# Four stages of a one-core transformer kernel recut: expert scaling on ScalarE, a convolution as TensorE products, and two reordered tails

## What is computed

```python
# layer 6: one of 8 experts per token
probs = softmax(xt @ router_w + router_b)
gate, idx = max(probs), argmax(probs)
y = gate[:, None] * (xt @ expert_w[idx] + expert_b[idx])

# layer 7: a memory trained by gradients along the sequence, chunks of 64 tokens
k, v, q = (causal_dwconv(hidden @ W.T, taps, bias) for each of three)   # 4 taps, 32 channels each
alpha, eta, theta = (mean over 32 gates of sigmoid or softplus) per token
per chunk: g = grad of |silu(k @ W1.T) @ W2.T - v|^2 at the chunk's start, clipped to norm 1
           S = eta*S - theta*g;  W = (1 - alpha)*W + S       # scan over the tokens
           retrieved = silu(q @ W1t.T) @ W2t.T
out = rmsnorm(retrieved @ Wo.T) * norm_g * (hidden @ gW.T + gb)
```

## Time and profile before

| | us |
|---|---|
| median of 3 runs | 3037.89 |
| lowest, highest | 3034.91, 3043.79 |
| the profiled execution | 3041.35 |
| its span (first to last instruction) | 3039.6 |
| busy over the span: TensorE, VectorE, ScalarE, GpSimd | 2865.2, 2198.7, 1436.9, 762.3 |
| stage l2_ffn | 53.4 |
| stage l3_prepare | 47.0 |
| stage l3_scan | 183.0 |
| stage l3_output | 22.9 |

### The profile page before, as it was taken

How to read it: one execution, slowest core, us unless ns; L and a number is a source line. 1 busy time by engine, 2 the same in 40 slices (tenths; PEclk the granted TensorE clock), 3 DMA queues, 4 the chain that set the end, 5 groups by cost and what they waited for, 6 DMA issues and landing times. The chain is left out here.

```text
span 3039.6 us, 43162 instructions
## 1 busy us (share of the span) xinstructions
PE 2865.2 (94%) x15588; PEld 1781.1 (59%) x15588; DVE 2198.7 (72%) x4611; ACT 1436.9 (47%) x2774; POOL 762.3 (25%) x680
## 2 busy tenths in 40 slices
PE   6999999999976999999999999999999887799698
PEld 4666666666643555555555555555555444466587
DVE  6888888888836877777777777777776467766655
ACT  3666666666641344444444444444444330433343
POOL 1000000000000344444444444444444310066200
PEclk7999999999996899999999999999999898655599
DMA  4121212121005011111101111101110000000000
GB/s 100 28 53 27 53 27 53 27 53 22 1 10 126 1 42 42 42 42 29 35 22 42 42 42 36 35 18 39 42 42 1 33 8 8 6 2 2 18 1 15
DMA packets 45476, 96.39 MB, mean 32 GB/s; under 512 B 13440, under 2 KB 33488, under 8 KB 37072
## 3 DMA queue, kind: packets, MB, share of 16 engines
q1 hardware_dynamic: 45264, 93.63, 13.5%
HBM read 35.67 MB, written 7.34 MB: 14 GB/s over the span
## 5 line engine op out<-in xcount | busy, mean ns | idle before, releaser
L963 ACT ACTIVATE l1a_PT<-l1a_st 128x512 f32<-128x512 f32 x1024 | 596.6, 598 | 760.7 <-PE l1a_st L879 756.5
L980 DVE TENSOR_REDUCE l1a_m<-l1a_aux 128x1 f32<-128x512 f32 x1024 | 667.0, 685 | 125.9 <-PE l1a_aux L841 123.8
L930 POOL TENSOR_TENSOR l1a_acc<-l1a_acc,l1a_PT 128x1024 f32<-128x1024 f32 x224 | 570.2, 2546 | 680.2 <-ACT l1a_PT L963 680.2
L465 DVE TENSOR_REDUCE l0s_mquad<-l0s_mx 128x1 f32<-128x512 f32 x1024 | 635.5, 683 | 142.7 <-PE l0s_mx L350 142.7
L440 ACT ACTIVATE l0s_PT<-l0s_st 128x512 f32<-128x512 f32 x1024 | 529.1, 602 | 274.3 <-PE l0s_st L366 271.6
L892 PE MATMUL l1a_ov<-l1a_PT,l1a_V 128*64 128x512 f32 x2048 | 495.7, 605 | 0.0
L877 PE MATMUL l1a_st<-l1a_QA,l1a_KA 128*128 128x512 f32 x1024 | 447.3, 437 | 2.3 <-issue 2.3
L366 PE MATMUL l0s_st<-l_QS,l_KS 128*128 128x512 f32 x1024 | 438.5, 431 | 5.3 <-DMA l_QS<-l0s_mrow 2.7
L350 PE MATMUL l0s_mx<-l_KS,l_QS 120*128 120x512 f32 x1024 | 417.7, 414 | 7.1 <-DMA l_QS<-qk_rows 7.0
L879 PE MATMUL l1a_st<-l1a_QB,l1a_KB 65*128 65x512 f32 x1024 | 405.9, 396 | 0.0
L841 PE MATMUL l1a_aux<-l1a_KA,l1a_QA 128*128 128x512 f32 x1024 | 399.0, 438 | 0.8 <-DVE l1a_lo L992 0.8
(11 more groups left out here) (349 smaller groups left out, 2642.4 us busy)
## 6 DMA issues: line engine op xcount, KB each, us to landing
l1a_KA<-l1a_hi SPq DMA_DIRECT2D x32, 512.0 KB, 8.2
l_KS<-qk_rows SPq DMA_DIRECT2D x64, 192.0 KB
l_QS<-qk_rows SPq DMA_DIRECT2D x128, 96.0 KB
l1a_QA<-l1a_hi SPq DMA_DIRECT2D x16, 512.0 KB, 4.5
l1a_QA<-l1a_lo SPq DMA_DIRECT2D x16, 512.0 KB, 8.6
l1a_QB<-l1a_hi SPq DMA_DIRECT2D x16, 512.0 KB, 4.5
l1a_KB<-l1a_lo SPq DMA_DIRECT2D x16, 512.0 KB, 6.4
qk_rows<-l0s_hi SPq DMA_DIRECT2D x64, 64.0 KB, 5.3
```

The lines of the kernel that those rows point to most:

```text
L465: nc.vector.tensor_reduce(mquad[:, u % 2, tile, g:g + 1], mx[:, n % MX0, :], axis=AX.X, op=ALU.max).then_inc(mx_free[n % MX0], 1)
L930: nc.gpsimd.tensor_tensor(acc[:, h % 2, 1, :], first, PT[:, g % PT_SLOTS, :], ALU.add).then_inc(added_pool, 1)
L963: nc.scalar.activation(PT[:, g % PT_SLOTS, (u % 2) * CW:(u % 2 + 1) * CW], st[:, u % ST1, :], ACT.Exp, scale=1.0 / float(np.sqrt(HD1))).th ...
L980: nc.vector.tensor_reduce(m4[:, b, q, c:c + 1], src, axis=AX.X, op=ALU.max).then_inc(aux_read, 1)
```

## The change

**l2_ffn.** The mask is made with a reduction and comparisons over all tiles at once instead of `max` and `max_index` per tile. The eight experts of a tile are split: four (`pv`) are added into X by VectorE as before, four (`pa`) are scaled by ScalarE into SBUF (`part`), and VectorE adds these in four wide additions per group. Six half-tiles are multiplied ahead of the mask instead of four.

```diff
-                for t in range(NT):
-                    nc.vector.max(top[:, t, :], probs[:, t, :]).then_inc(topped, 1)
-                for t in range(NT):
-                    dve.wait_ge(topped, t + 1)
-                    nc.vector.max_index(index[:, t, :], top[:, t, :], probs[:, t, :]).then_inc(topped, 1)
...
+                link(nc.vector.tensor_reduce(rowmax[:, :], probs[:, :, :], axis=AX.X, op=ALU.max))
+                link(nc.vector.tensor_tensor(e[:, :, :], probs[:, :, :], over_experts(rowmax[:, :]), ALU.is_lt))
+                link(nc.vector.scalar_tensor_tensor(e[:, :, :], e[:, :, :], float(E8), over_tokens(expert_no[:, :]),
+                                                    op0=ALU.mult, op1=ALU.add))
+                link(nc.vector.tensor_reduce(first[:, :], e[:, :, :], axis=AX.X, op=ALU.min))
...
+                    for i in range(HALF):
+                        nc.scalar.activation(part[:, c % 2, i, t % TPC, :], pa[:, t % 2, i * D:(i + 1) * D], ACT.Copy,
+                                             scale=mask[:, t, HALF + i:HALF + i + 1]).then_inc(scaled, 1)
...
+                        dve.wait_ge(scaled, HALF * TPC * (c + 1))
+                        for i in range(HALF):
...
+                            nc.vector.tensor_tensor(x, x, tiles(part[:, c % 2, i, :, :]), ALU.add).then_inc(summed, 1)
```

```diff
+            def convolve(c):
+                pe.wait_ge(taps_done, 1)
+                pe.wait_ge(eta_done, 2 * (c + 1))
+                nc.tensor.matmul(pb[0:R3, c, :], wt[:, TAPS - 1, :], xnT[:, cols(c)], start=True, stop=False)
+                for back in range(1, TAPS):
...
+            def rate():
+                pe.wait_ge(ln_done, 1)
+                pe.wait_ge(gate_read, 2)
...
-            nc.scalar.activation(gate_half[:, :], cw[:, 0:1], ACT.Tanh)
...
             nc.scalar.activation(T["Eend"][:, :], chunks(T["E"][MAIN, :])[:, :, CHUNK - 1], ACT.Copy)
+            nc.scalar.activation(gate_half[:, :], cw[:, 0:1], ACT.Tanh)
...
-            nc.gpsimd.tensor_tensor(ksq[:, :, :], T["ktok"][:, :, :], T["ktok"][:, :, :], ALU.mult).then_inc(ksq_done, 1)
```

```diff
                     nc.tensor.matmul(pred, state[:, c % 4, 1, 0, :], hd[:, c % 3, :], start=True, stop=True
                                      ).then_inc(s["pred_full"], 1)
                     if c >= 1:
-                        pe.wait_ge(s["tok_done"], 3 * c)
-                    if c >= 2:
-                        pe.wait_ge(s["m2_ready"], c - 1)
-                    nc.tensor.transpose(htok, hd[:, c % 3, :], ident[0:DM, 0:DM]).then_inc(s["htok_full"], 1)
+                        second_half_y1(c - 1)
...
                     nc.scalar.activation(e1[:, :], z, ACT.Tanh, scale=0.5).then_inc(s["e1_done"], 1)
...
+                    nc.scalar.activation(rest[:, :], e1[:, :], ACT.Identity, scale=-0.25, bias=quarter[:, :]
+                                         ).then_inc(s["rest_done"], 1)
...
+                    nc.scalar.activation(ckq[:, c % 2, :], T["CKQ"][:, at(c)], ACT.Copy, scale=thU[:, c:c + 1]
+                                         ).then_inc(s["ckq_done"], 1)
```

```diff
+            def gate(c):
+                dve.wait_ge(ms_done, TPC * (c + 1))
+                nc.vector.tensor_tensor(o[:, TPC * c:TPC * (c + 1), :], po[:, c, :].rearrange("p (t d) -> p t d", d=D),
+                                        T["gate"][:, TPC * c:TPC * (c + 1), :], ALU.mult).then_inc(gated, 1)
...
+                        nc.vector.scalar_tensor_tensor(X[:, t, :], o[:, t, :], inv[:, t:t + 1], X[:, t, :],
+                                                       op0=ALU.mult, op1=ALU.add).then_inc(added, 1)
-                    nc.vector.tensor_tensor(xt, xt, ot, ALU.add).then_inc(added, 1)
```

More of the change, by code:

```diff
@@ L1483, in l2_ffn @@
         norm(load)
+        HALF = E8 // 2
         probs = sb("probs", [P, NT, E8])
@@ L1579, in _ @@
                 dve.wait_ge(mask_done, 1)
                 adds = 0
[L1581 to L1585, removed]
+                for t in range(0, NT, 2):
+                    dve.wait_ge(pv_full, t + 2)
                     for i in range(HALF):
                         for j in range(2):
-                            t = units[u + j][0]
@@ L2100, in _ @@
             act.wait_ge(d1_set, 1)
             eta_of(0)
-            project(2)
+            gates(2)
             eta_of(1)
-            project(3)
+            convolved(0)
+            gates(3)
             eta_of(2)
+            act.wait_ge(tanh_done, NC)
+            nc.scalar.activation(tn[low, :], tn[low, :], ACT.Abs).then_inc(abs_done, 1)
+            convolved(1)
             eta_of(3)
-            for c in range(NC - 1):
-                query(c)
+            act.wait_ge(half_set, 1)
@@ L2109, in _ @@
+            act.wait_ge(abs_done, 1)
+            nc.scalar.activation(soft[3 * DM:4 * DM, :], tn[low, :], ACT.Ln, scale=0.5, bias=half[low, :]).then_inc(ln_done, 1)
             move(0)
-            for c in range(NC - 1):
-                value(c)
-            query(NC - 1)
-            act.wait_ge(half_set, 1)
-            act.wait_ge(abs_done, NC)
-            nc.scalar.activation(soft[3 * DM:4 * DM, :], tn[low, :], ACT.Ln, scale=0.5, bias=half[low, :]).then_inc(ln_done, 1)
-            nc.scalar.activation(gate_half[:, :], cw[:, 0:1], ACT.Tanh)
+            convolved(2)
@@ L2197, in _ @@
             scans(0)
-            conv(2)
             scans(1)
-            conv(3)
+            apart(0)
             scans(2)
             dve.wait_ge(gain_done, 2)
+            apart(1)
             gate(0)
             scans(3)
+            key_query(0)
             gate(1)
-            for c in range(NC):
-                key_query(c)
-            gate(2)
-            gate(3)
-            dve.wait_ge(ksq_done, 1)
-            nc.vector.tensor_reduce(T["k2"][:, :], ksq[:, :, :], axis=AX.X, op=ALU.add)
+            apart(2)
             dve.wait_ge(th_full, 1)
@@ L2215, in _ @@
                                         pp[e * CHUNK:(e + 1) * CHUNK, 1, 0:NT], -2.0 * GRAD_SCALE * LR3 / DM, None, ALU.mult)
+            apart(3)
+            key_query(1)
+            gate(2)
+            key_query(2)
+            gate(3)
+            dve.wait_ge(ksq_done, 2)
+            nc.vector.tensor_reduce(T["k2"][:, :], ksq[:, :, :], axis=AX.X, op=ALU.add)
+            key_query(3)
 def l3_scan(nc, ctx, T, ident, ones):
@@ L2284, in _, with second_half_y1 @@
         def _(pe):
+            def second_half_y1(o):
+                pe.wait_ge(s["second_coef"], o + 1)
+                pe.wait_ge(s["ckq_done"], o + 1)
+                nc.tensor.matmul(y1, dwe[:, o % 4, 0, :], ckq[:, o % 2, :], start=False, stop=True
+                                 ).then_inc(s["y1_full"], 1)
             for c in range(NCH + 2):
```

327 lines of the change are left out of this document (171 added, 156 removed).

## The result

The changed kernel took 3023.77 us (median of 4 runs, 3022.52 to 3024.02) where the kernel before took 3037.72 (4 runs, 3034.91 to 3043.79): a ratio of 0.9949, 95% interval 0.9934 to 0.9964. That is 14 us faster for a forecast of 13.2. A second set of runs gave 3023.18 and a ratio of 0.9956 (0.9942 to 0.9969). The total came out as forecast, but its parts did not: the scan's term was four times too small, and those of l2_ffn and l3_prepare were too large.

A forecast was written before the change was run, and what follows sets the result against it. Each stage had its own limit: VectorE in l2_ffn and l3_output, VectorE then TensorE in l3_prepare, a 5.51 us recurrence in l3_scan. -6.5 - 3.4 - 2.6 - 0.7 = -13.2 from 3037.89 gave 3024.7 us, range 3017 to 3035.

The forecast's parts named there:

- the scan's term: l3_scan: pred starts 0.15 us earlier, h2 ahead of dz leaves 0.08 a chunk over 32 chunks, -2.6 us.
- the root behind it is unchanged: l3_scan: gn comes at 2724.07 for 2724.15, and the root after it keeps its length.
- before they are needed: l3_scan: ScalarE's new steps and GpSimd's order end in time, slope 0.2 us earlier and `ckq` a chunk ahead.
- l3_prepare, -3.4 forecast: l3_prepare: TensorE becomes the bound, one half-speed stretch of 3.4 us loses 1.7, so 43.5 us for 46.9.
- full in the first half: l3_prepare before the change: TensorE's clock is full in the first half and 1.2 GHz after it.
- Rival (2): l3_prepare: the clock stays high, the stage gives 5.1 us, total 3023.0 us; chance 0.17.
- l2_ffn, -6.5 forecast: l2_ffn: mask 2.3 us earlier, TensorE the bound at 8.57 us a group, ScalarE's scaling hidden except 1.1 us; -6.5 us.
- l3_output, -0.7 forecast: l3_output: the wide addition of 0.69 us and its 0.03 go four times, four gate products come; -0.7 us.
- (1): l3_prepare: the clock stays low from the rates to the end, +6.3 us for -3.4, total 3034.4; chance 0.11.
- (4): l2_ffn: groups keep 9.24 us as engines hand each other banks, only the mask's 2.3 remain, total 3028.9; chance 0.09.
- (3): l3_scan: no gain, since h2 holds dz as long as pred was early, total 3027.3 us; chance 0.17.
- (5): l3_scan: early h2 lengthens each chunk, slower overall from 0.33 us a chunk, 3043 us at 0.5; chance 0.06.

The follow-up runs named there:

- experiment 9: Changed kernel with l3_prepare's rate passes one tile at a time among light products, the one-column Tanh behind the Ln, and h2 back behind `side`: 3024.78 us.
- Experiment 2: Kernel before with only GpSimd's list in l3_scan changed (`ckq` moved to ScalarE), VectorE's and TensorE's orders kept: 3032.7 us.
- experiment 4: Changed kernel with four more GpSimd products, into a buffer nobody reads, behind the third base in l3_scan: 3027.9 us.
- experiment 8: Changed kernel with the 32 rate passes moved to the end of TensorE's work in l3_prepare: 3015.82 us, ratio 0.992 to the kernel before.
- experiment 1: Kernel before with the changed l3_scan alone: 3031.24 us, ratio 0.9969.

## Why the prediction was right or wrong

**The total** was right (3024.7 for 3023.8), in part by luck: -13.2 was made of terms whose errors cancel.

**l3_scan, -2.6 forecast, -10.5 measured.** The step that failed is the sentence that gn comes earlier and "the root behind it is unchanged". The front half was right in size: pred came 0.16 earlier (0.15 forecast), and gn at 3.14 for 3.21 behind z (0.08 forecast). But h2 did not hold dz: dz started 0.13 behind h2, not 0.18, and kept the 0.15 (2.14 behind z for 2.29). The 0.07 were lost behind the norm of dz: from its first pass to gn it takes 0.50 us in the mean for 0.41, and 0.45 with h2 back in its old place (experiment 9). Why is open, and that the two sizes agree is luck. But the root's own operations were taken as fixed costs, and three of them contained a wait for GpSimd that no idle time shows, since it lies within their duration. It was 0.25 us a chunk, 7.9 in all. Experiment 2 took it away, and experiment 4 brought two thirds of it back. The evidence stood in rows already quoted: the forecast itself said of l3_prepare that a scan was stretched from 1.23 to 2.94 us while GpSimd squared the keys. It then wrote GpSimd's new order off as ending "before they are needed", and did not ask beside which VectorE work it ran.

**l3_prepare, -3.4 forecast, -1.9 in the two traces, nothing in the time.** The clock's fall within or behind the rates was forecast and came. Its size was the first wrong term: 3.4 us at half clock and 1.7 lost were assumed, 6.8 us and some 3.5 lost were measured. It was also not the only fall: the second, at 2642.5, made the last key-query products take 1.58 us for 1.13, beside ScalarE's reads. The second error is the base. The prediction's reading of it, "full in the first half", is rough too: PEclk was 0.50 up to 2610.4, 1.00 from 2611 to 2624 and 0.50 from there on, though the sum did price the start at 1.2 GHz. 46.9 us was one execution's length of a stage that also takes 42.3, and 3.5 us for the first projections at half clock was carried over, where the first trace of the changed kernel shows 1.93. The third are the light products: the forecast priced eight passes of 128 columns at 0.95 and 0.90 by passes of eight columns, and at the full clock they take 1.09, seven times on the path, 1.1 us in all. Rival (2), that the clock stays high, did not happen. The rule that was read that way (the Trainium skill, TensorE: Matmul & The Clock Gate, What's actually happening: the clock falls after idling) does not cover what the traces show, a fall while TensorE was busy all the time (experiment 8, 6.20 of 6.20 us and 5.80 of 5.80 around it).

**l2_ffn, -6.5 forecast, -5.5 measured.** TensorE as the bound, the mask 2.3 us earlier, and ScalarE's scaling hidden were right: 1.15 us a tile, for 1.1. The term that was short is the group: 8.72 for 8.57, three times, 0.45 us; the products take 0.1 longer behind the transposes too. The last bias products then waited 0.38 us until ScalarE had copied the mask behind its scaling. Together 0.8 of the 1.0. The advice of the Trainium skill (ScalarE: Activation LUTs, Rules for kernel authors) to multiply on VectorE did not hold here: the 64 scalings lie beside TensorE's work, and their 1.15 us a tile cost no more than that 0.38 us.

**l3_output, -0.7 forecast, -1.0 measured.** The traces show 29.9 to 30.2 us with the new code and 30.9 to 31.5 with the old.

**The rivals.** (1) and (4) did not happen. Nor did (3): with the new orders alone dz kept its 0.15, and the front half gave some 0.07 a chunk. (5) put the price of an early h2 at 0.33 us a chunk and more; it is 0.05 (experiment 9).

## What to carry to other kernels

In a chain of short VectorE operations, look at what GpSimd does beside each of them, and compare the duration of the same operation where GpSimd is idle: a wait of this kind shows as length and never as idle time. Where thin TensorE passes stand ahead of heavy ones on the path, try them at the end, where another engine's tail covers them: here that gave 5.8 us of the stage, and mixing them among light products cost 3 to 4. A stage whose length depends on where the granted clock falls has no single length: before costing an edit of a few us there, look at more than one execution.

## What the runs showed of the hardware

- A VectorE step of 64x1 with both tensor inputs in SBUF takes 0.15 us alone and 0.23 to 0.25 when it starts with that much of a GpSimd operation of 0.31 still to run, and ends 0.01 to 0.02 behind it. One that starts with 0.06 left keeps its 0.14, and dz, with an input in PSUM, its 0.21 with 0.30 left.
- The granted clock was 0.50 through 16.00 us in which TensorE was busy for 16.00, with one-column passes between products of 128 columns and transposes (experiment 9). Products of the same kinds without them ran at 1.00 for 6.20 us (experiment 8), but in the changed kernel the clock fell to 0.50 at 2642.5 behind some 5.9 us of them too (from 2636.56), with TensorE busy throughout. So no run singles out the one-column passes as the cause.
- The same instructions of two stages took 93.2 and 99.6 us in two executions (experiment 1's, and the kernel before), with the granted clock placed differently.
